# Splitting the shared expert's down products of steps 8 to 18, with GpSimd computing the low part

## The reference

```
x = x + attn_a(layernorm(x))
x = x + ffn(layernorm(x))
x = x + attn_b(layernorm(x))
x = x + ffn(layernorm(x))

def _swiglu(x, gate_up, down):                  # I = 938
    h = einsum('bsd,fd->bsf', x, gate_up)       # 128 -> 2 * I
    g, u = split(h, 2, axis=-1)
    return einsum('bsi,di->bsd', silu(g) * u, down)   # I -> 128

out = _swiglu(x, shared_gate_up, shared_down)   # the shared expert, for all tokens
probs = softmax(einsum('bsd,ed->bse', x, gate_weight))   # E = 8
top_p, sel = top_k(probs, 2)                    # normalised to sum 1
for e in range(E):
    out = out + cw[..., e:e + 1] * _swiglu(x, experts_gate_up[e], experts_down[e])
```

## Time and profile before

| | us |
|---|---|
| median of three runs | 998.67 |
| their range | 996.67 to 999.59 |
| the profiled execution, its time | 1006.71 |
| its span, first to last instruction | 1004.4 |
| PE busy | 957.7 |
| DVE busy | 722.4 |
| POOL busy | 616.2 |
| ACT busy | 568.1 |

### The profile page before, as it was taken

One profiled execution on the slowest core, in us unless ns is written; L12 is line 12 of the kernel. 1 busy time (PEld: TensorE's weight loads), 2 busy tenths in 40 slices (PEclk: granted clock), 3 DMA queues, 4 the chain that ended last, 5 costly groups with the idle time before them and its releaser, 6 DMA issues. The chain is left out here.

```text
span 1004.4 us, 16126 instructions
## 1 busy us (share of the span) xinstructions
PE 957.7 (95%) x4711; PEld 678.4 (68%) x4711; DVE 722.4 (72%) x1192; ACT 568.1 (57%) x1046; POOL 616.2 (61%) x482
## 2 busy tenths in 40 slices
PE   7999999898899998999999999999999999999997
PEld 3323333232366797999999556667666999999996
DVE  3999998999678665566665697776597666666665
ACT  6664655655442554555554698787733555555553
POOL 1599897999630967854642378963305777667432
PEclk9899979999999999999999999999999999999999
DMA  5323223363250233222000400000702222411104
GB/s 157 66 73 86 74 76 74 85 108 94 87 158 26 62 87 94 75 73 76 28 33 17 119 24 1 2 1 1 224 0 71 66 79 62 131 62 39 33 24 132
DMA packets 69247, 69.70 MB, mean 69 GB/s; under 512 B 14952, under 2 KB 51568, under 8 KB 69168
## 3 DMA queue, kind: packets, MB, share of 16 engines
q1 hardware_dynamic: 64176, 58.44, 20.6%
q0 software_dynamic: 4992, 10.23, 3.9%
HBM read 58.00 MB, written 10.62 MB: 68 GB/s over the span
## 5 line engine op out<-in xcount | busy, mean ns | idle before, releaser
L810 POOL TENSOR_TENSOR a_hc<-a_h,a_c_sb 128x512 f32<-128x512 f32 x128 | 159.4, 1267 | 49.1 <-DVE a_h L711 48.9
L492 PE MATMUL ps<-a_hc,eye 128*128 128x512 f32 x256 | 135.2, 642 | 12.9 <-POOL a_hc L810 12.2
L629 ACT ACTIVATE ps<-a_delta,a_neg_a 128x512 f32<-128x512 f32 x128 | 87.0, 689 | 72.2 <-DVE a_h L711 70.5
L492 PEld LDWEIGHTS ps<-a_hc,eye 128*128 128x128 f32 x256 | 45.5, 196 | 82.6 <-POOL a_hc L810 42.2
L711 DVE TENSOR_TENSOR_SCAN a_h<-ps,a_state,a_b_u 128x512 f32<-128x512 f32 x64 | 78.7, 1266 | 1.6 <-POOL a_hc L810 0.8
L1214 PE MATMUL ps<-f_ring_rounded,f_q_hi_rounded 128*128 x312 | 77.0, 337 | 1.3 <-DVE f_q_hi_rounded L1746 1.3
L1214 PE MATMUL ps<-g_ring_rounded,g_q_hi_rounded 128*128 x312 | 77.1, 337 | 0.1
L711 DVE TENSOR_TENSOR_SCAN a_h<-ps,a_b_u 128x512 f32<-128x512 f32 x64 | 75.1, 1207 | 2.8 <-ACT ps L629 2.7
L1067 POOL DMA_INDIRECT g_rows<-xn_rows,g_source x39 | 37.2, 954 | 56.1 <-DVE g_source L1700 35.4
L1067 POOL DMA_INDIRECT f_rows<-xn_rows,f_source x39 | 37.3, 956 | 52.9 <-DVE f_source L1700 35.5
L691 DVE TENSOR_TENSOR a_b_u<-a_du,ps 128x1024 f32<-128x1024 f32 x57 | 68.1, 1195 | 1.6 <-PE ps L479 1.5
(11 more groups left out here) (486 smaller groups left out, 2740.3 us busy)
## 6 DMA issues: line engine op xcount, KB each, us to landing
a_c_sb<-c_rows SPq DMA_DIRECT2D x64, 256.0 KB, 3.4
f_ring<-in_gu SPq DMA_DIRECT2D x16, 469.0 KB
g_ring<-in_gu SPq DMA_DIRECT2D x16, 469.0 KB
f_ring<-in_dn SPq DMA_DIRECT2D x8, 512.0 KB
g_ring<-in_dn SPq DMA_DIRECT2D x8, 512.0 KB
xn_rows<-f_work SPq DMA_DIRECT2D x8, 256.0 KB, 4.0
f_rows<-token_rows SPq DMA_DIRECT2D x8, 256.0 KB, 4.6
xn_rows<-g_work SPq DMA_DIRECT2D x8, 256.0 KB, 4.0
```

The costliest lines, as they stand in the source:

```text
L492: nc.tensor.matmul(ps[:, Y + f, :], k.eye[:, :], hc[:, s % WAITING, :], start=False, stop=(n == NST - 1)).then_inc(y_added, 1)
L629: nc.scalar.activation(ps[:, A + m % NA, :], delta[:, f, cols(g)], ACT.Exp, scale=neg_a[:, f, n:n + 1])\
L810: nc.gpsimd.tensor_tensor(hc[:, m % WAITING, :], h[:, s % DEPTH, :], c_sb[:, i % RING, :], ALU.mult)\
```

## The change

Steps 8 to 18 get the form that steps 19 and later have. `POOLED = 8` marks the first of them. For these eleven steps, in each of the two stages: DVE writes the product to `whole_at(q, m)`, four quarters of `work` used in turn, where the token rows were; before step 8 it waits until all token rows are stored, and from step 12 on until GpSimd has read the quarter. ACT rounds it into `q_hi`. GpSimd subtracts `q_hi` from it into `q_lo` and counts `pool_ready` (the old `both_ready` under a new name). PE waits for that and does three rounded products in place of the float32 one. GpSimd's eleven subtractions stand in its list between the split of expert 1 and the waits ahead of the first gather.

```diff
--- before.py
+++ after.py
@@ -900,13 +900,13 @@
         tokens_copied, rows_stored, step, exp_ready, chosen_ready, counts_ready, spots_ready, found_ready, \
         source_ready, share_ready, table_ready, w_high, w_ready, g_ready, gu_ready, silu_done, prod_done, high_ready, \
         low_ready, summed, x_added, rest_zero, x_turned, xt_high, xt_low, gates_ready, ups_ready, gates_silu, \
-        prods_ready, prods_turned, q_high, q_low, cross_ready, outs_ready, both_ready, tokens_ready, out_added, \
+        prods_ready, prods_turned, q_high, q_low, cross_ready, outs_ready, pool_ready, tokens_ready, out_added, \
         stored = sems(
             "plain_loaded centred squared var_ready log_done rstd_ready normed x_high x_low logits_ready tokens_turned "
             "tokens_copied rows_stored router_step exp_ready chosen_ready counts_ready spots_ready found_ready "
             "source_ready share_ready table_ready w_high w_ready g_ready gu_ready silu_done prod_done high_ready "
             "low_ready summed x_added rest_zero x_turned xt_high xt_low gates_ready ups_ready gates_silu "
-            "prods_ready prods_turned q_high q_low cross_ready outs_ready both_ready tokens_ready out_added "
+            "prods_ready prods_turned q_high q_low cross_ready outs_ready pool_ready tokens_ready out_added "
             "stored")
     if following is not None:
         next_centred, next_squared, next_var, next_loaded, next_log, next_rstd = sems(
@@ -923,6 +923,7 @@
     NQ = NCH * TILES
     LAST_ROWS = UT + 2
     PLAIN, COUNT, FIND, SOURCES = 19, 7, 19, 19
+    POOLED = 8
     done = 0 if logs is not None else ready
     CENT = (0, 1, 2, 3) if logs is None else (0, 1, 4, 7)
     VAR = (5, 6, 7, 4) if logs is None else (5, 6, 3, 1)
@@ -937,6 +938,12 @@
 
     def split(n):
         return max(0, n - PLAIN)
+
+    def highs(n):
+        return max(0, n - POOLED)
+
+    def whole_at(q, m):
+        return work[0:m, (q % 4) * CH:(q % 4 + 1) * CH]
 
     L = EXPERTS
     N = TT * EXPERTS
@@ -1057,6 +1064,11 @@
 
             for part in range(PARTS):
                 split_part(1, part)
+            for q in range(POOLED, PLAIN):
+                m = k_of(q % TILES)
+                pool.wait_ge(high_ready, highs(q + 1))
+                nc.gpsimd.tensor_tensor(p_at(q_lo, q, m), whole_at(q, m), p_at(q_hi, q, m).bitcast(F32), ALU.subtract)\
+                    .then_inc(pool_ready, 1)
             pool.wait_ge(k.first_row, 16)
             pool.wait_ge(rows_stored, 16 * TOP * NCH)
             pool.wait_ge(source_ready, 1)
@@ -1083,7 +1095,7 @@
                 pool.wait_ge(out_loaded[g], 16 * TOP)
                 part = slice(4 * g, 4 * g + 4)
                 nc.gpsimd.tensor_tensor(both[:, 0, part, :], both[:, 0, part, :], both[:, 1, part, :], ALU.add)\
-                    .then_inc(both_ready, 1)
+                    .then_inc(pool_ready, 1)
             if following is not None:
                 pool.wait_ge(next_loaded, 64)
                 nc.gpsimd.tensor_scalar(following.w_in[:, :], following.w_in[:, :], k.vec[:, VB_NORM:VB_NORM + 1],
@@ -1163,12 +1175,15 @@
                     pe.wait_ge(tokens_copied, NCH)
                 if q == 2 * TILES:
                     pe.wait_ge(x_added, 1)
-                if q < PLAIN:
+                if q < POOLED:
                     pe.wait_ge(prod_done, q + 1)
                     nc.tensor.matmul(ps[:, SUMS[c], :], plain_dn[:, i, :], p_at(norm_sq, q, P),
                                      start=(i == 0), stop=(i == TILES - 1)).then_inc(summed, 1)
                     return
-                pe.wait_ge(low_ready, split(q + 1))
+                if q < PLAIN:
+                    pe.wait_ge(pool_ready, q + 1 - POOLED)
+                else:
+                    pe.wait_ge(low_ready, split(q + 1))
                 product(ps[:, SUMS[c], :], k.sh_dn[:, i, 0, :], k.sh_dn[:, i, 1, :],
                         p_at(q_hi, q, P), p_at(q_lo, q, P), i == 0, i == TILES - 1).then_inc(summed, 1)
 
@@ -1300,7 +1315,7 @@
             gate_up(NPRE + 1)
             down_tile(SLOT_TILES - 1)
             def turn_rows(g):
-                pe.wait_ge(both_ready, g + 1)
+                pe.wait_ge(pool_ready, PLAIN - POOLED + g + 1)
                 if g >= 2:
                     pe.wait_ge(out_added, g - 1)
                 for t in range(4):
@@ -1387,7 +1402,8 @@
                     act.wait_ge(summed, q - 3)
                 if q >= NPRE:
                     act.wait_ge(summed, SLOT_TILES + max(NPRE, q - 3))
-                nc.scalar.activation(p_at(q_hi, q, m), up_at(q, m), ACT.Copy).then_inc(high_ready, 1)
+                whole = whole_at(q, m) if q < PLAIN else up_at(q, m)
+                nc.scalar.activation(p_at(q_hi, q, m), whole, ACT.Copy).then_inc(high_ready, 1)
 
             def evac(j):
                 for half in range(2):
@@ -1449,7 +1465,7 @@
                     split_x(1)
                 if q == 3:
                     exponentials()
-                if PLAIN < q < NPRE - 1:
+                if POOLED < q < NPRE - 1:
                     high(q - 1)
                 if 0 < q < NCH:
                     copy_tokens(q)
@@ -1717,14 +1733,18 @@
                     up = ps[UT:UT + TAIL, G + q % 2, :]
                 if split(q - 2):
                     dve.wait_ge(low_ready, split(q - 2))
-                if 4 <= q < PLAIN:
+                if 4 <= q < POOLED:
                     dve.wait_ge(summed, q - 3)
-                to = p_at(norm_sq, q, m) if q < PLAIN else up_at(q, m)
+                if q == POOLED:
+                    dve.wait_ge(rows_stored, 16 * TOP * NCH)
+                if POOLED + 4 <= q < PLAIN:
+                    dve.wait_ge(pool_ready, q - 3 - POOLED)
+                to = p_at(norm_sq, q, m) if q < POOLED else whole_at(q, m) if q < PLAIN else up_at(q, m)
                 nc.vector.tensor_tensor(to, gate_at(q, m), up, ALU.mult).then_inc(prod_done, 1)
 
             def low(q):
                 m = k_of(q % TILES)
-                dve.wait_ge(high_ready, split(q + 1))
+                dve.wait_ge(high_ready, highs(q + 1))
                 nc.vector.tensor_tensor(p_at(q_lo, q, m), up_at(q, m), p_at(q_hi, q, m).bitcast(F32), ALU.subtract)\
                     .then_inc(low_ready, 1)
 

```

## The result

The changed kernel takes 1031.47 us (median of four executions: 1019.53, 1024.13, 1038.80, 1039.38) against 999.02 us (the kernel before, now with a fourth execution), 3.2% by the medians. The forecast was 1008.1 us, range 1001.5 to 1012.5: right in direction, wrong in size.

The account below looks back on a forecast made before the run. DVE's chain ahead of find_tokens was taken to bound the kernel. Blocking by GpSimd delays find_tokens 5.0 us, less 0.3 saved behind it: 4.7 per stage, 9.4 on 998.67, so 1008.1 us, range 1001.5 to 1012.5.

Parts of the forecast that it names:

- Who bounds: Steps 8 to 19: DVE's chain sets find_tokens' start; PE gains ahead of it are lost unless DVE ends sooner.
- PE's saving of 0.3 us behind find_tokens: Triples of steps 17 and 18, behind find_tokens, save 0.3 us per stage, the only sure part of PE's gain.
- Exclusion: Two-input DVE operations and POOL subtractions block each other, 0.15 us overlap at each change; 5.3 us for the eleven subtractions.
- low(11): Step 11's subtraction, followed by a PSUM-reading operation and a product, 1.2 us of free cover: cost 0.
- low(9): Step 9's subtraction, taken as about like those followed by a product: delay 0.46 us.
- the 0.3 us of idle time: DVE idle time in steps 8 to 19, ahead of L1666, taken to absorb 0.3 us of the delay.
- The stored rows: Step 8's product waits for the stores, landed at 289.6, almost seven us before its turn: cost 0.
- ACT: Eleven roundings of 0.59 us, 6.5 us on top of 7.67 in 25.6, nothing on the path: cost 0.
- POOL's list: Subtractions stand ahead of the gathers, but the first gather waits for find_tokens' result anyway: cost 0 there.
- Rival 5: PE waits for low(q), some 3 us from product q's end; near, but no price of its own; no chance given.
- Two stages with the same rows: 2 x 4.7: Sum: both stages lose 4.7 us each, 9.4 us in all, giving 1008.1 us.
- The range: Whole time 1001.5 to 1012.5 us, reaching into rival 3 (light contention, 1000.7), leaving out rivals 1, 2, most of 4.

Follow-up runs that it names:

- e3_no_pool: Changed kernel without GpSimd's eleven subtractions, the middle product reading the high part instead; executions 996.0, 1009.9, 1011.6 and 1028.1 us.
- e4_pool_alone: Kernel before plus GpSimd subtractions with unused results behind the products of steps 8 to 18; 1035.99 us, ratio 1.0382.
- e2_before_table_early: Kernel before with the whole expert table behind product 19, nothing else changed; 997.72 us, ratio 0.9995.
- e1_table_early: Changed kernel with all six pieces of the expert table behind product 19, instead of three there and three behind step 20; 1013.11 us, ratio 1.0137.
- e13_from_11: Changed kernel with POOLED = 11, so steps 8 to 10 keep their float32 down; 1021.79 us, ratio of the two shorter executions 1.0113.
- e5_quarter: Changed kernel with GpSimd's subtractions of steps 12 to 18 cut to 128 of 512 columns; 1006.35 us, ratio 1.0085.
- e9_low_on_dve: Changed kernel with the subtractions of steps 8 to 18 on VectorE, none on GpSimd; 1029.54 us, ratio of the two shorter executions 1.0174.

## Why the prediction was right or wrong

- **Who bounds.** Right. VectorE's chain sets find_tokens, and PE's 1.4 us saved ahead of it only became a wait (1.44 us in e3_no_pool).
- **PE's saving of 0.3 us behind find_tokens.** Consistent: find_tokens +5.9, tile +5.6 in stage g.
- **Exclusion.** Right in kind and price: POOL's work 1.29 us (1.27 taken), 0.4 to 0.5 under a product, 1.0 to 1.1 otherwise, nothing for low(11). Two terms were mis-sized. low(9), put at 0.46 under a product, met the small two-input L1656 and cost 1.1. And the 0.3 us of idle time that were to absorb a part absorbed nothing: VectorE still has 30.10 - 29.73 = 0.37 us of it in the longer stretch, and I read them as gaps between dependent instructions, not slack. 5.0 + 0.6 + 0.3 = 5.9, as measured.
- **The stored rows, ACT, POOL's list.** Nothing there, as said; e3_no_pool has the first two, and is at 26.1.
- **Rival 5.** PE did wait for low(q), up to 0.57 us at a time; without any such wait (e4_pool_alone) find_tokens is at 31.7, so it has no price of its own, or one of 0.3 us (the subtractions of that kernel also come a rounding earlier).
- **The step that failed: "Two stages with the same rows: 2 x 4.7", with everything behind find_tokens moved as a block.** I had noted that PE would idle ahead of L1185 and asked of it only how long. I should have asked what PE does after being idle, and what is late next. A wait of 1.4 us there was followed by TensorE's lower clock in some stages; step 20's product then came 1.7 us later against the gathers, and the table's cast with it; and that cast must be through before GpSimd's fourth gather is well begun. In the kernel before, the first cast does so with 1.15 us to spare (327.22 against 328.37); in the changed kernel it comes 0.51 us behind the gather's start (334.41 against 333.90). These are the rows of the kernel before (VectorE, then GpSimd), the table's three casts, the third and the fourth gather and the first of the weight instructions:

```profile
327.22 0.16 DVE L1686 CAST f_table<-f_found 1x39 int32<-1x39 f32 x1
...
327.77 0.29 DVE L1690 CAST f_table<-f_tiles 1x8 int32<-1x8 f32 x1
327.88 0.21 DVE L1693 CAST f_table<-f_found 1x39 int32<-1x39 f32 x1
...
327.13 0.94 POOL L1067 DMA_INDIRECT f_rows<-xn_rows,f_source  x1 [0.30 <-issue]
328.37 0.95 POOL L1067 DMA_INDIRECT f_rows<-xn_rows,f_source  x1 [0.30 <-issue]
329.33 1.77 POOL L1047 CAST f_ring_rounded<-f_ring 128x1876 fp32r<-128x1876 f32 x1
```

  The sign was already there. L1690 and L1693 begin 0.64 and 0.75 us into the third gather and end with it (328.06 and 328.09 against 328.07), in 0.29 and 0.21 us where e2_before_table_early, with no gather beside them, has 0.15 and 0.17: the gather held them. Behind the third gather GpSimd pauses for 0.30 us, behind the fourth it goes on without a gap (334.84, 334.85 in the changed kernel). That the missing gap is why the cast then loses to the weight instructions too is read from these rows, no run tests it.
  The clock's fall costs 3 to 5 us a stage (e1_table_early), the cast some 9 (8.76 us of PE's waiting), together about the 12.7 of stage f. A stage with the router's delay and both follow-ups loses 17 to 20 us in the profiled executions, where 4.7 were forecast.
- **The range.** It held the router's delay with all bounds of its unknown price, and no bound for what a new wait may set off. With both follow-ups mended the same change is at 1008.24, inside the range; of that the nearness to 1008.1 is luck, as said.

## What to carry to other kernels

When a change makes a full engine wait, price the wait, and then look behind it: which instructions are now late against an engine that was not delayed, and is any of them a VectorE operation that GpSimd, with several instructions in a row, is about to hold up? Before moving work to an idle GpSimd, count how many two-input VectorE operations stand beside it, since here eleven such subtractions cost VectorE as much as doing them itself. If executions of one kernel differ by steps of equal size, look for a stall that either happens or not, stage by stage, before blaming the chip.

## What the runs showed of the hardware that was not expected

- A cast on VectorE from SBUF to SBUF of only 39 or 8 numbers waited 9.4 to 9.8 us in eight stages of five profiled executions, each time to the end of four GpSimd instructions in a row (in the changed kernel L1054, L1056, L1059, L1062). It did not get in between them, as the two-input L1520 had between L1047 (over at 280.92) and L1049.
- How far into a gather such a cast can begin is not told by one number. Ahead of the weight instructions, those that began 0.09 to 0.15 us into the gather took 0.16 us, and those from 0.32 us on (e13_from_11, stage g) were held. In gathers with a pause behind them, casts that began up to 0.48 us in took 0.15 to 0.17 us, and those from 0.57 us on ended with the gather, after 0.21 to 0.37 us. Which part of a gather holds VectorE is open.
- The Trainium skill ("SBUF — State Buffer", section "Who interferes with whom") has the loser blocked for the other's whole instruction. This agrees with most single meetings; the cast here lost four times in a row, and in e5_quarter a GpSimd subtraction of 0.46 us lost to a router piece that began 0.58 us after its own row, and took 2.37 us. What decides who goes first after such a wait stays open.
- TensorE's granted clock fell to the lower level behind an idle time of 1.43 to 2.66 us ahead of find_tokens in ten profiled stages (f of the changed kernel and of e3_no_pool, both of e1_table_early, e13_from_11, e9_low_on_dve and e4_pool_alone) and did not behind 1.45 us in two (g of the first two). An idle time of 1.54 us at another place (e5_quarter, 310.96 to 312.50) was followed by full clock. With the idle time ahead of find_tokens filled by seven small matmuls it did not fall there in either stage of the two profiled executions. What tips it in one stage and not in the other is open.
